# Cross attention of the second layer: every projection in three passes of high and low parts, with the parts made by ScalarE and VectorE

## The reference, cut to what matters

```python
def _L1_xattn_ref(q, k, v, mask, w_q, w_k, w_v, out_w, out_b):
    ...
    fq = (q @ w_q).reshape(batch, seq_q, HEADS, ATTN).transpose(0, 2, 1, 3)
    fk = (k @ w_k).reshape(batch, seq_k, HEADS, ATTN).transpose(0, 2, 1, 3)
    fv = (v @ w_v).reshape(batch, seq_k, HEADS, ATTN).transpose(0, 2, 1, 3)
    f = jnp.einsum('bhqd,bhkd->bhqk', fq, fk) / jnp.sqrt(jnp.float32(ATTN))
    f = f + jnp.where(mask == 0, jnp.float32(-1000000000.0), jnp.float32(0.0))
    ps = jax.nn.softmax(f, axis=-1)
    attns = jnp.einsum('bhqk,bhkd->bhqd', ps, fv)
    attns = attns.transpose(0, 2, 1, 3).reshape(batch, seq_q, HEADS * ATTN)
    return attns @ out_w.T + out_b
```

## Time and profile before

| what | value |
| --- | --- |
| median of 3 runs | 3266.99 us (3266.16 to 3267.48) |
| profiled execution, its own time | 3266.41 us |
| its span in the trace | 3264.6 us |
| mean granted clock of PE | 0.911 |
| PE busy | 2818.9 us, 86% of the span |
| DVE, ACT, POOL busy | 1942.7 us, 1693.0 us, 694.7 us |
| the stage's first matmul and its last addition to x start at | 2462.47 us and 2890.66 us |

### The profile page before, as it was taken

How to read it: one execution, slowest core, us unless ns; L and a number is a source line. 1 busy time by engine, 2 the same in 40 slices (tenths; PEclk the granted TensorE clock), 3 DMA queues, 4 the chain that set the end, 5 groups by cost and what they waited for, 6 DMA issues and landing times. The chain is left out here.

```text
span 3264.6 us, 49578 instructions
## 1 busy us (share of the span) xinstructions
PE 2818.9 (86%) x16640; PEld 2049.9 (63%) x16640; DVE 1942.7 (60%) x4248; ACT 1693.0 (52%) x3120; POOL 694.7 (21%) x806
## 2 busy tenths in 40 slices
PE   6788888888855559999997999999989999949998
PEld 3344444444334436766765888888886777738887
DVE  4778777877754346556644566565664454444444
ACT  3887888788842224444443555555555555542221
POOL 1122222222110004444451000000003565620000
PEclk9889988998776669999998999999998999979999
DMA  2000000000000020110012000000001000020000
GB/s 98 4 4 4 0 3 3 3 0 3 1 17 26 25 67 23 28 40 22 23 22 57 1 1 1 1 1 1 1 26 64 7 3 6 4 88 7 6 6 29
DMA packets 87121, 59.37 MB, mean 18 GB/s; under 512 B 54688, under 2 KB 76576, under 8 KB 86496
## 3 DMA queue, kind: packets, MB, share of 16 engines
q1 hardware_dynamic: 87008, 57.89, 5.9%
HBM read 41.10 MB, written 8.39 MB: 15 GB/s over the span
## 5 line engine op out<-in xcount | busy, mean ns | idle before, releaser
L1820 POOL TENSOR_SCALAR x_weights<-x_weights,x_sums 128x256 f32<-128x256 f32 x256 | 231.7, 923 | 884.0 <-DVE x_sums L1857 884.0
L670 DVE SCALAR_TENSOR_TENSOR a_w<-a_w,a_sinks 128x384 f32<-128x384 f32 x512 | 332.8, 715 | 31.5 <-ACT a_w L505 31.5
L1074 POOL TENSOR_SCALAR f_weights<-f_weights,f_sums 128x256 f32<-128x256 f32 x256 | 232.1, 924 | 271.5 <-DVE f_sums L1304 271.5
L484 ACT ACTIVATE a_e<-psum 128x1024 f32<-128x1024 f32 x192 | 195.3, 1017 | 158.0 <-PE psum L343 118.7
L1506 ACT ACTIVATE a_turned_w_hi<-psum 128x512 fp32r<-128x512 f32 x256 | 139.0, 595 | 195.2 <-PE psum L1440 195.1
L1232 ACT ACTIVATE f_weights<-psum,f_negmax 128x256 f32<-128x256 f32 x256 | 117.8, 472 | 215.5 <-DVE f_negmax L1298 215.5
L685 DVE SCALAR_TENSOR_TENSOR a_w<-a_e,psum 128x512 f32<-128x512 f32 x256 | 162.8, 677 | 96.1 <-ACT a_e L486 86.5
L340 PE MATMUL psum<-a_qT,a_kT_half 32*128 32x512 f32 x512 | 166.3, 729 | 60.6 <-DVE a_w L685 48.8
L1570 DVE TENSOR_REDUCE a_negmax<-psum 128x1 f32<-128x1024 f32 x128 | 156.7, 1224 | 89.8 <-PE psum L123 89.8
L486 ACT ACTIVATE a_e<-a_e 128x1024 f32<-128x1024 f32 x192 | 202.9, 1057 | 6.1
L1790 ACT ACTIVATE x_weights<-x_masked_s,x_negmax 128x256 f32<-128x256 f32 x256 | 126.9, 496 | 146.4 <-DVE x_negmax L1853 146.3
(11 more groups left out here) (305 smaller groups left out, 7092.7 us busy)
## 6 DMA issues: line engine op xcount, KB each, us to landing
x_ctxT<-in_x_ctxT SPq DMA_DIRECT2D x16, 256.0 KB, 2.7
f_xnT<-all_xnT_all SPq DMA_DIRECT2D x16, 256.0 KB, 2.3
f_pv_rows<-f_pv SPq DMA_DIRECT2D x8, 512.0 KB, 3.1
f_pv_groups<-f_pv_rows SPq DMA_DIRECT2D x8, 512.0 KB
f_w<-in_f_w SPq DMA_DIRECT2D x2, 2048.0 KB, 10.1
all_x_all<-in_x SPq DMA_DIRECT2D x1, 2048.0 KB, 8.9
a_wq<-in_a_wq SPq DMA_DIRECT2D x2, 1024.0 KB, 9.4
a_wo<-in_a_wo SPq DMA_DIRECT2D x2, 1024.0 KB, 12.2
```

The lines of the kernel that those rows point to most:

```text
L484: act.activation(e[:, x, :], psS[x], ACT.Exp).then_inc(exp_done, 1)
L670: ins = dve.scalar_tensor_tensor(part, part, sinks[:, col:col + 1], part, ALU.is_ge, ALU.mult)
L1074: ins = pool.tensor_scalar(w, w, sums[:, k, h, t:t + 1], None, ALU.mult)
L1820: ins = pool.tensor_scalar(w, w, sums[:, k, h, t:t + 1], None, ALU.mult)
```

## The change

The stage's projections all use `split_product`, so each matmul of float32 becomes three of float32r. For that each operand is held as a high part (rounded to float32r) and a low part (what is left).

- The weights' parts are made at the head, by ACT (`weights_high`, a copy) and DVE (`weights_low`, a subtraction). The raw weights are loaded into tiles that the stage uses only later: `weights`, `v` and `turned_w`.
- The parts of the rows of x (`x_split`, `x_rest`) and of the context (`ctx_split`, `ctx_rest`) are made batch by batch, in steps 0 and 1 for the batch that follows. The context is no longer loaded as a whole. SP brings one batch of it at a time into `ctx_raw`.
- The result of a pair is written to `oT` as two parts, both by DVE: a copy, a wait for it, and a subtraction.
- The loop of the sequencers is gone. `each_batch` writes out all batches.
- PE waits for the parts (`w_low`, `x_low`, `ctx_low`). The wait for all loads moves from PE to ACT.

```diff
--- before.py
+++ after.py
@@ -1633,6 +1633,12 @@
...
+def each_batch(eng, body):
+    for b in range(-1, B + 1):
+        body(b, 0 <= b < B, b + 1 < B, b >= 1)
...
@@ -1640,29 +1646,37 @@
...
-        wq, wk, wv = (s.sb(n, [P, CC, HD]) for n in ("wq", "wk", "wv"))
-        wo, bo = s.sb("wo", [P, HD // P, D]), s.sb("bo", [P, D])
-        mask_i, mask = s.sb("mask_i", [P, TT, T], I32), s.sb("mask", [P, TT, T])
-        ctxT_all, ctxT = s.sb("ctxT_all", [P, B, CC, T]), s.sb("ctxT", [P, CC, T])
+        halves = lambda name, shape: [s.sb(f"{name}_{part}", [P] + shape, F32R) for part in ("hi", "lo")]
+        wq, wk, wv = (halves(n, [CC, HD]) for n in ("wq", "wk", "wv"))
+        wo, bo = halves("wo", [HD // P, D]), s.sb("bo", [P, D])
+        mask = s.sb("mask", [P, TT, T])
+        xT, ctxT, ctx_raw = halves("xT", [CC, T]), halves("ctxT", [2, CC, T]), s.sb("ctx_raw", [P, CC, T])
...
+        mask_i = masked_s[:, 0, 0].bitcast(I32)
...
-        oT = s.sb("oT", [P, PAIRS, T])
+        oT = halves("oT", [PAIRS, T])
...
+        w_high, w_low, x_high, x_low, ctx_high, ctx_low, oT_high = (
+            s.sem(n) for n in ("w_high", "w_low", "x_high", "x_low", "ctx_high", "ctx_low", "oT_high"))
         x_biased, out_ready, out_taken, pool_passed = (
             s.sem(n) for n in ("x_biased", "out_ready", "out_taken", "pool_passed"))
-        loads = [(wk[:], chunked(a["wk"])), (wq[:], chunked(a["wq"])),
-                 (ctxT_all[:], a["ctxT"].rearrange("(b k p) n -> p b k n", k=CC, p=P)), (wv[:], chunked(a["wv"])),
-                 (wo[:], chunked(a["wo"])), (bo[:], over_partitions(a["bo"], D)), (mask_i[:], chunked(a["mask"]))]
+        raw = [weights[:, 2 * i:2 * i + 2].rearrange("p r h t n -> p r (h t n)") for i in range(2)] + \
+              [v[:], turned_w[:].rearrange("p r h t n -> p (r h t n)").rearrange("p (k n) -> p k n", n=D)]
+        loads = [(raw[0], chunked(a["wq"])), (raw[1], chunked(a["wk"])), (raw[2], chunked(a["wv"])), (raw[3], chunked(a["wo"])),
+                 (bo[:], over_partitions(a["bo"], D)), (mask_i, chunked(a["mask"]))]
...
@@ -1675,16 +1689,14 @@
...
-            with sp.Fori(0, B) as b:
-                sp.wait_ge(v_ready, b * V)
-                sp.dma_start(ctxT[:], a["ctxT"][bass.ds(b * D, D), :].rearrange("(k p) n -> p k n", p=P))\
+            for b in range(B):
+                if b >= 1:
+                    sp.wait_ge(ctx_low, b)
+                sp.dma_start(ctx_raw[:], a["ctxT"][b * D:(b + 1) * D, :].rearrange("(k p) n -> p k n", p=P))\
...
-            pe.wait_ge(loaded, 16 * len(loads))
...
@@ -1694,17 +1706,22 @@
...
+                    if i % 2:
+                        pe.wait_ge(w_low, 2)
+                        pe.wait_ge(ctx_low, bb + 1)
+                    else:
+                        pe.wait_ge(w_low, 1)
+                        pe.wait_ge(x_low, bb + 1)
...
-                            src = (xnT_all, ctxT_all)[i % 2][:, bass.ds(bb, 1), c, :]
-                            ins = pe.matmul(qk_bank(i)[:, j * T:(j + 1) * T], (wq, wk)[i % 2][:, c, lo:lo + P], src,
-                                            start=(c == 0), stop=(c == CC - 1))
+                            ins = split_product(pe, qk_bank(i)[:, j * T:(j + 1) * T], [z[:, c, lo:lo + P] for z in (wq, wk)[i % 2]],
+                                                [z[:, bb % 2, c, :] for z in ctxT] if i % 2 else [z[:, c, :] for z in xT], c == 0, c == CC - 1)
...
-                        pe.wait_ge(ctx_here, bb * 16 + 16)
+                        pe.wait_ge(w_low, 3)
...
@@ -1715,18 +1732,19 @@
...
-                        ins = pe.matmul(v_bank(i), ctxT[:, c, t * P:(t + 1) * P], wv[:, c, half * HALF:(half + 1) * HALF],
-                                        start=(c == 0), stop=(c == CC - 1))
+                        ins = split_product(pe, v_bank(i), [z[:, bb % 2, c, t * P:(t + 1) * P] for z in ctxT],
+                                            [z[:, c, half * HALF:(half + 1) * HALF] for z in wv], c == 0, c == CC - 1)
...
+                        pe.wait_ge(w_low, 4)
...
-                        ins = pe.matmul(out_bank(i), oT[:, k, i * P:(i + 1) * P], wo[:, k, :], start=(k == 0),
-                                        stop=(k == PAIRS - 1))
+                        ins = split_product(pe, out_bank(i), [z[:, k, i * P:(i + 1) * P] for z in oT],
+                                            [z[:, k, :] for z in wo], k == 0, k == PAIRS - 1)
...
@@ -1772,15 +1790,40 @@
...
-            over_batches(pe, body)
+            each_batch(pe, body)
...
+            act.wait_ge(loaded, 16 * len(loads))
+            def weights_high(w, n):
+                act.activation(w[0][:], raw[n], ACT.Copy).then_inc(w_high, 1)
+            def x_split(bb):
+                wait(act, qk_ready, (bb - 1) * QK + 7)
+                act.activation(xT[0][:], xnT_all[:, bb], ACT.Copy).then_inc(x_high, 1)
+            def ctx_split(bb):
+                act.wait_ge(ctx_here, bb * 16 + 16)
+                wait(act, v_ready, (bb - 1) * V)
+                act.activation(ctxT[0][:, bb % 2], ctx_raw[:], ACT.Copy).then_inc(ctx_high, 1)
...
+                    if b == -1 and p == 0:
+                        weights_high(wq, 0)
+                    if b == -1 and p == 1:
+                        weights_high(wk, 1)
+                    if b == -1 and p in (3, 4):
+                        weights_high(wv if p == 3 else wo, p - 1)
+                    if ahead and p == 0:
+                        ctx_split(b + 1)
+                    if ahead and p == 1:
+                        x_split(b + 1)
...
@@ -1804,7 +1847,7 @@
...
-            over_batches(act, body)
+            each_batch(act, body)
...
@@ -1825,20 +1868,38 @@
...
-            over_batches(pool, body)
+            each_batch(pool, body)
...
-            step.link(dve.tensor_copy(mask[:], mask_i[:]))
+            step.link(dve.tensor_copy(mask[:], mask_i))
             step.link(dve.tensor_scalar(mask[:], mask[:], 0.0, MASKED, ALU.is_equal, ALU.mult))
+            def weights_low(w, n):
+                dve.wait_ge(w_high, n + 1)
+                dve.tensor_tensor(w[1][:], raw[n], w[0][:].bitcast(F32), ALU.subtract).then_inc(w_low, 1)
+            def x_rest(bb):
+                dve.wait_ge(x_high, bb + 1)
+                dve.tensor_tensor(xT[1][:], xnT_all[:, bb], xT[0][:].bitcast(F32), ALU.subtract).then_inc(x_low, 1)
+            def ctx_rest(bb):
+                dve.wait_ge(ctx_high, bb + 1)
+                dve.tensor_tensor(ctxT[1][:, bb % 2], ctx_raw[:], ctxT[0][:, bb % 2].bitcast(F32), ALU.subtract).then_inc(ctx_low, 1)
...
+                    if b == -1 and p == 0:
+                        weights_low(wq, 0)
+                    if b == -1 and p == 1:
+                        weights_low(wk, 1)
+                    if b == -1 and p in (3, 4):
+                        weights_low(wv if p == 3 else wo, p - 1)
...
@@ -1851,6 +1912,10 @@
...
+                    if ahead and p == 0:
+                        ctx_rest(b + 1)
+                    if ahead and p == 1:
+                        x_rest(b + 1)
...
@@ -1878,9 +1943,15 @@
...
-                        dve.tensor_copy(oT[:, k, :], psum[:, O0, 0:T]).then_inc(oT_ready, 1)
-            over_batches(dve, body)
+                        if k == 0:
+                            wait(dve, out_ready, (n // PAIRS - 1) * OUT + 2)
+                        dve.tensor_copy(oT[0][:, k, :], psum[:, O0, 0:T]).then_inc(oT_high, 1)
+                        dve.wait_ge(oT_high, n + 1)
+                        dve.tensor_tensor(oT[1][:, k, :], psum[:, O0, 0:T], oT[0][:, k, :].bitcast(F32), ALU.subtract)\
+                           .then_inc(oT_ready, 1)
+            each_batch(dve, body)
...
```

## The result

The changed kernel takes 3283.95 us (median of 5 runs, 3278.52 to 3285.27). The kernel before, beside it, takes 3267.48 us. The ratio is 1.0049, with a 95% interval of 1.0034 to 1.0064: slower by half a per cent. The forecast was 3284 us.

A forecast was written before the change was run, and what follows sets the result against it. PE was the bound, by only 1.5 us in six steps over the DVE and ACT chain. Head +13, batch 0 +0.6, six batches -2.6, end -2.4, clock +8 gave +17 us: 3284 us, range 3270 to 3297.

The forecast's parts named there:

- head: Stage start to first maxima: 11.5 to 13.5 us later as parts are made first; 13 taken.
- batch 0: First batch: +0.46 us in each of steps 5 to 7, -0.8 in step 4, together +0.6.
- six batches, without the clock: Six batches at -0.43 us each, -2.6 in all, leaving out clock falls.
- falls of the clock: Half clock after the idle time ahead of each output projection: 0.7 x 1.65 us, seven times, 8 us.
- last batch and end: -0.8 us for v, -2.6 for two output projections, +1.0 for two low parts: -2.4.
- The bound: Steps 5 to 2: DVE and ACT chain, 33.8 of 35.3 us, grows 2.8 by oT's low part; PE bounds steps 3, 4.
- PE's gain: Three float32r passes save PE 5.4 us a batch, of which 0.4 arrive.
- The idle time: PE idles some 3 us in one piece ahead of each output projection, waiting for the last oT low part.
- Rival 1: Clock doesn't fall at the new gaps ahead of the output projection: +9 us, 3276; chance 0.22.
- Rival 2: PE stays the bound and its gain arrives, -5.4 us in each of six batches: 3243 us; chance 0.12.
- Rival 3: Full 1.65 us lost at each output projection and again in steps 7 to 1 or by late code: 3299; chance 0.13.
- The loop written out: Batch loop unrolled: counted as nothing, bounds a gain of 1 us and a loss of 1.65 each batch.

The follow-up runs named there:

- the pair's result first: Changed kernel with DVE's copy and subtraction for oT ahead of PE's work beside the pair, outside steps 3 and 4: 3254.35 us, ratio 0.9959 to the kernel before.
- the head in float32 products: Changed kernel with oT's low part one step later and the first six q and k products on raw float32 tiles: 3261.8 us, 0.9985 of before.

## Why the prediction was right, and where it was not

The total was forecast to 0.1 us, and this is partly luck. The pieces, in us:

| term | predicted | measured in the profile |
| --- | --- | --- |
| head | +13 | +14.2 |
| batch 0 | +0.6 | +1.7 |
| six batches, without the clock | -2.6 | -1.0 |
| falls of the clock | +8 | +2.9 |
| last batch and end | -2.4 | -1.8 |
| sum | +16.6 | +16.0 |

- **The bound.** Right. The chain through DVE and ACT had 1.5 us of room in six steps, and the low part took 2.8. The steps are 5.69 and 6.28 us, with 5.7 and 6.3 predicted. The experiments pin it from both sides: 0.33 us more on DVE in each step arrive in full, 3.5 us more on PE in 50 don't arrive at all, and with the low part in DVE's wait the steps are 5.23 and 5.82 again.
- **PE's gain.** Mis-sized by 0.7 us: I had 5.4. When PE is the bound again a batch takes 47.2 us with 49.63 of 50 busy, 46.9 of work, so three passes save 4.7 us in a batch. The rows below show half of what is missing. A product of v behind one of q took 1.71 us and takes 1.40. The four in a batch save 1.3 us where I had 1.66: I took the old price from the pair in step 4, which stands behind scores and has the slower start described next in it, and the new price from neighbours of one kind. The output projection takes 5.78 us where I had 5.71. The first matmul of a product behind scores is slower (0.21 us pass ahead of it and 0.22 behind it, where neighbours of one kind have 0.12), but so it was before (2673.89 to 2674.10, and 1.83 us for such a product in place of 1.73), so three passes neither add to it nor take from it. None of it changes the sum, since the gain wasn't to arrive. The first four rows are of before, the others of after.

```profile
2673.89 0.28 PE L1745 MATMUL psum<-x_kT_hi,x_qT_lo 64*128 64x256 f32 x2
2674.10 1.99 PE L1701 MATMUL psum<-all_xnT_all,x_wq 128*128 x8
2675.93 1.88 PE L1718 MATMUL psum<-x_wv,x_ctxT 128*128 128x512 f32 x4
2677.64 1.04 PE L1759 MATMUL psum<-all_ident,x_weights 128*128 128x128 f32 x8
...
2644.45 0.28 PE L1763 MATMUL psum<-x_kT_hi,x_qT_lo 64*128 64x256 f32 x2
2644.66 0.39 PE L121 MATMUL psum<-x_xT_hi,x_wq_hi 128*128 128x256 f32 x1
2644.88 0.28 PE L122 MATMUL psum<-x_xT_lo,x_wq_hi 128*128 128x256 f32 x1
...
2685.03 0.40 PE L121 MATMUL psum<-x_wv_hi,x_ctxT_hi 128*128 128x512 f32 x1
...
2686.43 1.03 PE L1777 MATMUL psum<-all_ident,x_weights 128*128 128x128 f32 x8
```

- **Six batches.** The chain of six steps was 36.5 and is 36.5 (2 x 5.69 + 4 x 6.28). Step 3 was 9.0 and is 9.1, step 4 5.6 and is 5.75. These two are PE's, and came out 0.25 us long together.
- **The idle time.** Right in place and size: 3.09 us, up to the last low part, and gone when that part is made earlier (the pair's result first). The Trainium skill (TensorE: Matmul & The Clock Gate, Why this matters for your kernels) warns of such gaps. The prediction took from it that equal gaps cost every time or never; two of six did here, so what it took from the page did not hold.
- **The clock.** The term that was mis-sized. I gave a fall 0.7 of seven chances. There were only six such gaps: in the last batch PE waits 0.13 us ahead of the projection of step 3 and 1.02 ahead of the very last one. The fall came in two of the six in both profiles, at 1.5 us (1.65 predicted). This term was 5.1 us too large, and the other four were together 4.5 us too small, which is why the sum came out. The other kernels show that 0.7 was no worse a guess than 0.3: four, five or six of six fell there, after idle times of 2.02 and 3.87 us. So the three gaps in before's trace could not give the chance, and a range was the right answer. Rival 1 (3276) and the forecast differed by this term alone, and the profile lies nearer to rival 1 in it.
- **The head.** 27.7 us after the block's start, where 26.4 was predicted. PE started after 8.1 us (8.4 predicted) and the third low part was finished after 20.8 (20.6 predicted), so the order of the parts and the wait of 4.52 us for a bank are as reckoned. The piece that was mis-sized is the last: the two remaining products ran wholly at half clock (granted clock 0.50), and the first maxima came 6.8 us after the first of them started. I had reckoned 4.2 to 6.2 and taken a value between. That the parts ahead of and between the products make the head long is shown by the head in float32 products, 2.1 us longer than before's in place of 14.2.
- **Batch 0.** Steps 5 to 7 cost 1.3 us by the chain, as predicted. Step 4 gave back 0.4 and not 0.8. What I had left out is step 3: it took 0.8 longer, at a granted clock of 0.50 after 2.77 us of idle time, where before's had 0.61 after 2.47 us. Where the clock stayed up, the same step was 2.4 us shorter (3.46 against 5.90).
- **Rival 2**, PE as the bound with its gain arriving, was excluded by the order of DVE's instructions, and so it was: with that order changed it came true, at batches of 47.57 us. Rival 3 had a second fall in each batch; no profile has one outside step 3 in batches 1 to 6. The loop written out is nothing.

## What to carry to other kernels

A busy share of 100% says which engine is the bound now, and not by how much. Before making its work cheaper, add up the next chain in the rows without idle time, here 33.8 of 35.3 us, and put whatever the cheaper form asks of the other engines onto that chain. If it doesn't fit, look for the wait within the chain: an instruction placed into it was free here, and the same instruction some 1.4 us earlier, ahead of the next maxima, cost its whole length. Parts of weights that every first product waits for are a fixed price; whatever can start on the raw tiles should.

## What the hardware showed that I had not expected

- Whether the clock falls isn't told by the length of the idle time alone. After 2.02 us it fell in nine of twelve batches, after 3.05 to 3.09 in four of twelve, after 1.63 in three of six, after 3.87 in six of six, after 0.82 in none of six. Identical gaps in one execution had both outcomes. The counts are small, and the batches of one execution follow each other at equal distances, so they may not be independent; they are no chances to reckon with. Under 1 us there was no fall. What decides it from 1.6 to 3.1 us is open.
- What an idle time costs comes behind it: 2.02 us of waiting, which were hidden themselves, brought 1.5 us at half clock on the path.
- Stages that were not changed have two lengths. `attention1` took 692.4 to 692.9 us in seven profiles and 696.6 to 696.7 in five, and the last stage 344.2 to 344.9 in eight and 346.6 to 347.5 in four, in no relation to the kernel. So two single profiles that differ by 4 us in total say little, and a stage should be compared by itself.
